# A new order of every engine's tasks, and weight preparation laced with the first image

## The chip, the cores and the metric

The kernel runs on one core of a Trainium2 chip. Its time is in microseconds (us) of the device, from launch to end. The kernel before was timed in 3 runs: median 3233.88, from 3227.86 to 3242.86.

## The reference

Sixteen images x of 512 channels and 32x32 pixels go through self-attention over their 1024 pixels, with 8 heads of width 64:

```python
h = jnp.einsum('oc,bcn->bno', wp, xf)            # wp: 1536x512, rows normalised
qkv = h.reshape(B, N, n_heads, 3 * d_k)
q, k, v = jnp.split(qkv, 3, axis=-1)
q = pixnorm(q) * scale                            # x / sqrt(mean(x*x) + eps)
k = pixnorm(k) * scale
v = pixnorm(v)
attn = jnp.einsum('bihd,bjhd->bijh', q, k)
attn = jax.nn.softmax(attn, axis=2)
res = jnp.einsum('bijh,bjhd->bihd', attn, v)
res = jnp.einsum('oc,bnc->bon', wo, res.reshape(B, N, C))   # wo: 512x512, normalised
return (a_c * x + b_c * res) / div
```

## The kernel before

Every factor of a product is split into a high and a low part, and three products (high-high, high-low, low-high) are summed. Each engine runs one fixed list of tasks, and semaphores count how many tasks of each kind are done. For one image the tasks are:

- TensorE (PE): `project` n = 0..23 (12 matmuls into one of two banks of `ps_dense`), `score` m = 0..31 (12 matmuls, two slots of 128 keys by 512 queries and two heads), `attend` m = 0..31 (48 matmuls, the same two slots into `ps_pv`), `project_out` k = 0..7 (12 matmuls, again a bank of `ps_dense`). A slot is t = 2m or 2m+1; 64 slots make an image, 8 a unit (`take`), 16 a pair of heads.
- ScalarE (ACT): `square` and `copy_proj` of each `project`; `exp` of each slot; `high_probs` of the slots with t % 8 in (1, 4, 6); the high parts of x, v, q and k, and of the result; `finish` of the output.
- VectorE (DVE): `reduce`, `seed_norms`, `scale`; `split_probs_high` of the other 40 slots (line 619) and `split_probs_low` of all 64 (line 628); the low parts; `take_pv`; `add_out`.
- GpSimd (POOL): `norms`, 14 dependent steps for each of 3 groups of `project`.
- SyncE (SP): loads, stores and the transposing DMAs `turn_qk` and `turn_res`, in one queue.

What follows from the buffers: `exp` of slot t needs the scores of t and the low part of slot t-2 (two `e_tile`); the scores of slot t need `exp` t-2 (two slots of `ps_score`); a high part of slot t needs `attend` of slot t-4 (four `probs`), counted by the finished pair of slots (`VISITS`); a matmul group in a bank of `ps_dense` needs the `copy_proj` or `add_out` of the group before it in that bank (`bank_free`). The chain of a slot is score, exp, high part, low part, attend.

The order is a set of hand-over tables: each task has a tick in a period of 4096 ticks, negative or above 4095 where it runs in the period of the image before or after. `timeline` walks the ticks, and only their order on an engine matters. So in one pass of the loop an engine works for three images: late tasks of b-1 (below with a minus, as out0-), those of b, early ones of b+1 (with a plus). Images 1 to 14 are the loop; image 0's early part, and the last two passes, are written out. Before all this stands the preparation of 16 tiles of weights, stage after stage: all 16 loaded and squared, one chain of norms, 16 scaled, then turned on PE, split by ACT and DVE (lines 513 to 526, 700 to 730, 836 to 845).

```python
SCORE_AT = (-42, 56, 141, 572, 697, 817, 936, 1056, ...)
PROB_BUFS = 4
VISITS = SLOTS // 2
```

## Time and profile before

| | us |
|---|---|
| median of the runs shown | 3233.88 (3227.86 to 3242.86) |
| time of the profiled execution | 3256.49 |
| span of its profile, first to last instruction | 3254.4 |
| PE busy in the span | 3027.5 (93%) |
| DVE busy | 2666.0 (82%) |
| ACT busy | 2304.7 (71%) |
| POOL busy | 335.8 (10%) |

The profiled execution is 0.7% longer than the median of the others. Matmuls are pipelined, so that the durations of neighbours overlap: how long a task holds PE is read from the start of one task to the start of the next. "Idle before" is the time in which the engine did nothing before a row, with the instruction that ended it. The clock column is the share of TensorE's full clock that was granted.

### The profile page before, as it was taken

The numbers are of one execution on the slowest core, as the hardware profiler recorded it, in microseconds if no ns is written. First come the engines' busy times: TensorE is split into PE (matmuls) and PEld (weight loads), VectorE is DVE, ScalarE is ACT, GpSimd is POOL, SyncE is SP. The second block draws the span as 40 slices with busy tenths as digits, with TensorE's granted clock in tenths as the row PEclk, the third lists the DMA queues.
The fourth block names the chain that finished last, engine by engine and source line by source line (L and its number), as shares of the span: only waits on it lengthen the run. The fifth ranks groups of instructions, "written<-read, shape, count | busy, mean of one in ns | idle before, by whom it ended". The sixth has DMA issues, their size and how long they took to land.

```text
span 3254.4 us, 91845 instructions
## 1 busy us (share of the span) xinstructions
PE 3027.5 (93%) x36928; PEld 2060.7 (63%) x36928; DVE 2666.0 (82%) x3295; ACT 2304.7 (71%) x2865; POOL 335.8 (10%) x678
## 2 busy tenths in 40 slices
PE   4899999999999899999989999899999999999987
PEld 3666666766667566666666667566665666667653
DVE  3788787888879888797888878788897887878875
ACT  4677676767767777676777767677776776767664
POOL 0120100201102011100201002011010201002010
PEclk9999999999999999999999999999999999999999
DMA  2312323124142321323223232231423223232232
GB/s 78 62 42 49 90 48 92 41 60 94 36 102 44 80 63 38 102 48 83 49 57 90 43 99 36 69 81 35 108 40 83 57 48 91 48 92 41 50 79 59
DMA packets 459635, 212.11 MB, mean 65 GB/s; under 512 B 407953, under 2 KB 407953, under 8 KB 459153
## 3 DMA queue, kind: packets, MB, share of 16 engines
q1 hardware_dynamic: 459152, 205.58, 28.0%
q8 instruction: 315, 5.16, 0.7%
q14 instruction: 168, 1.37, 0.1%
HBM read 71.30 MB, written 33.55 MB: 32 GB/s over the span
## 4 chain that ended last, share of the span: by engine, by line
issue 77%; POOL 10%; PE 5%; DVE 5%; ACT 1%; DMA 1%; POOLq 1%; SPq 0%; DVEq 0%; ACTq 0%
POOL rs L323 3%; POOL rs_t L319 2%; POOL rs_t L317 2%; POOL rs_t L321 2%; DVE probs L628 2%; PE ps_pv L799 1%; DVE probs L619 1%; PE ps_dense L758 1%; PE ps_score L778 1%; PE ps_dense L762 1%; PE ps_dense L760 1%; POOL sumsq L314 1%; ACT e_tile L456 1%; DVE arena L590 0%; ACT probs L463 0%
## 5 line engine op out<-in xcount | busy, mean ns | idle before, releaser
L456 ACT ACTIVATE e_tile<-ps_score,shift 128x1024 f32<-128x1024 f32 x1024 | 1109.3, 1113 | 316.3 <-PE ps_score L778 183.2
L628 DVE TENSOR_TENSOR probs<-e_tile,probs 128x1024 f16<-128x1024 f32 x1024 | 1242.0, 1226 | 56.4 <-ACT probs L463 47.1
L799 PEld LDWEIGHTS ps_pv<-v_pair,probs 128*128 128x128 f16 x24576 | 804.2, 98 | 297.8 <-DVE probs L628 145.6
L799 PE MATMUL ps_pv<-v_pair,probs 128*128 128x65 f16 (+1 forms) x24576 | 863.1, 194 | 119.6 <-DVE probs L628 87.6
L778 PE MATMUL ps_score<-qkT 64*128 64x512 f16 x6144 | 762.1, 381 | 6.8 <-ACT e_tile L456 3.9
L619 DVE CAST probs<-e_tile 128x1024 f16<-128x1024 f32 x640 | 442.2, 693 | 247.2 <-ACT e_tile L456 241.4
L758 PE MATMUL ps_dense<-wpT_hi,x_hi 128*128 128x512 f32 x1536 | 629.9, 410 | 8.4 <-DVE x_lo L557 7.0
L762 PE MATMUL ps_dense<-wpT_hi,x_lo 128*128 128x512 f32 x1536 | 601.9, 392 | 0.0
L760 PE MATMUL ps_dense<-wpT_lo,x_hi 128*128 128x512 f32 x1536 | 600.2, 391 | 0.0
L778 PEld LDWEIGHTS ps_score<-qkT 64*128 64x128 f16 x6144 | 257.6, 95 | 312.7 <-issue 42.6
L416 ACT ACTIVATE squares<-ps_dense 128x512 f32<-128x512 f32 x384 | 228.1, 594 | 277.4 <-PE ps_dense L762 277.4
L463 ACT ACTIVATE probs<-e_tile 128x1024 f16<-128x1024 f32 x384 | 405.9, 1057 | 15.0 <-PE ps_pv L799 0.2
L758 PEld LDWEIGHTS ps_dense<-wpT_hi,x_hi 128*128 128x128 f32 x1536 | 288.7, 188 | 145.8 <-issue 81.6
L566 DVE TENSOR_REDUCE sumsq<-squares 128x8 f32<-128x512 f32 x384 | 261.7, 681 | 103.6 <-ACT squares L416 93.8
L762 PEld LDWEIGHTS ps_dense<-wpT_hi,x_lo 128*128 128x128 f32 x1536 | 288.8, 188 | 64.2
L760 PEld LDWEIGHTS ps_dense<-wpT_lo,x_hi 128*128 128x128 f32 x1536 | 289.7, 189 | 53.1
L314 POOL TENSOR_TENSOR sumsq<-sumsq,shift 128x64 f32<-128x64 f32 x48 | 19.7, 411 | 2761.7 <-DVE rs L534 2761.7
L590 DVE TENSOR_TENSOR arena<-arena,rs 128x1024 f32<-128x1024 f32 x192 | 228.8, 1221 | 34.4 <-POOL rs L325 34.4
L483 ACT ACTIVATE x_res<-x_res 128x512 f32<-128x512 f32 x128 | 80.7, 630 | 244.3 <-DVE x_res L655 244.3
L815 PE MATMUL ps_dense<-resT,woT_hi 128*128 128x512 f16 x512 | 207.0, 404 | 48.6 <-ACT arena L426 44.2
L426 ACT ACTIVATE arena<-ps_dense 128x512 f32<-128x512 f32 x384 | 225.6, 592 | 0.2 <-DVE arena L610 0.2
L816 PE MATMUL ps_dense<-resT,woT_hi 128*128 128x512 f16 x512 | 205.6, 402 | 0.0
(50 smaller groups left out, 1765.7 us busy)
## 6 DMA issues: line engine op xcount, KB each, us to landing
x_raw<-in_x SPq DMA_DIRECT2D x128, 256.0 KB, 3.0
x_res<-in_x SPq DMA_DIRECT2D x128, 256.0 KB, 2.7
out<-x_res SPq DMA_DIRECT2D x128, 256.0 KB, 2.5
arena<-in_w_proj SPq DMA_DIRECT2D x24, 128.0 KB, 2.6
qkT<-arena SPq DMA_TRANSPOSE x128, 4.3
resT<-res_split SPq DMA_TRANSPOSE x128, 3.1
arena<-in_w_out SPq DMA_DIRECT2D x1, 1024.0 KB, 5.7
```

What stands on the lines that cost most here:

```text
L416: act.activation(squares[:, n % 2, :], ps_dense[:, PROJ_BANK[n], :], ACT.Square).then_inc(squared, 1)
L456: act.activation(e_tile[:, t % 2, :, :], ps_score[:, t % 2, :, :], ACT.Exp, bias=shift[:, 0:1], scale=1.0 / (QK_UP * QK_UP)).then_inc(exp_ ...
L463: act.activation(probs_of(b, t, 0), e_tile[:, t % 2, :, :], ACT.Copy).then_inc(probs_high_act, 1)
L566: dve.tensor_reduce(sumsq[:, g, nt, :], squares[:, n % 2, :].rearrange("p (g d) -> p g d", d=D), AX.X, ALU.add).then_inc(reduced, 1)
L590: dve.tensor_tensor(v, v, r, ALU.mult).then_inc(scaled, 1)
L619: dve.tensor_copy(probs_of(b, t, 0), e_tile[:, t % 2, :, :]).then_inc(probs_high, 1)
L628: dve.tensor_tensor(probs_of(b, t, 1), e_tile[:, t % 2, :, :], probs_of(b, t, 0), ALU.subtract).then_inc(probs_low, 1)
L758: pe.matmul(ps_dense[:, bank, :], x_hi[:, ct, pix], wpT_hi[:, ct, cols], start=(ct == 0), stop=False)
L760: pe.matmul(ps_dense[:, bank, :], x_hi[:, ct, pix], wpT_lo[:, ct, cols], start=False, stop=False)
L762: mm = pe.matmul(ps_dense[:, bank, :], x_lo[:, ct, pix], wpT_hi[:, ct, cols], start=False, stop=(ct == CT - 1))
L778: mm = pe.matmul(ps_score[:, t % 2, h, :], k[rows, k_part, :], q[rows, :, q_part, :], start=(i == 0), stop=(i == 2))
L799: mm = pe.matmul(ps_pv[:, h, o:o + n], probs_of(b, t, part)[:, h, queries], v[:, cols], start=(j == 0 and it == 0 and part == 0 and cols.s ...
```

## The change

Three things change, and no operation of an image's work does.

1. All tables of the period are new. On PE one pass of the loop reads, before:

```
attend31- score1 attend0 score2 proj14 proj15 proj16 proj17 proj18 proj19 attend1 score3 proj20 attend2 score4 out0- attend3 score5 out1- attend4 score6 out2- ... (score, dense, attend by turns) ... attend26 score28 attend27 score29 attend28 score30 attend29 score31 attend30 score0+
```

and now:

```
attend29- score31- proj13 score0 attend30- attend31- score1 proj14 proj15 proj16 score2 attend0 attend1 score3 proj17 score4 attend2 proj18 attend3 score5 out0- out1- proj19 attend4 score6 out2- ... proj9+ attend23 score25 proj10+ score26 attend24 attend25 score27 proj11+ score28 attend26 attend27 score29 proj12+ score30 attend28
```

`PROJ_BANK` and `OUT_BANK` swap most banks. The tables of the other engines follow.

2. The weights go through in three chains (tiles 0 to 3, 4 to 7, 8 to 15), and their tasks stand in one list with image 0's early tasks (tables `FIRST_..._AT` and `W_..._AT`). The turned weights use all four banks of `ps_score`, squares two scratch tiles. `first` adds waits for image 0: a projection for the weights it reads, a copy into the arena for the tile it overwrites, the first score for all 16.

3. `pv_done` goes up for each slot, not for each two.

```diff
+W_CHAINS = ((0, 4), (4, 8), (8, 16))
-SCORE_AT = (-42, 56, 141, 572, 697, 817, 936, 1056, 1175, 1300, 1420, 1540, 1659, 1779, 1904, 2029, 2154, 2279,
+SCORE_AT = (19, 56, 248, 278, 829, 866, 988, 1012, 1363, 1379, 1439, 1537, 1643, 1667, 1693, 1854, 1898, 2312,
...
-PROJ_BANK = (0, 1, 0, 1, 0, 1, 0, 1, 0, 1, 0, 1, 0, 1, 0, 1, 0, 1, 0, 1, 0, 1, 0, 1)
-OUT_BANK = (1, 0, 1, 0, 0, 1, 0, 1)
+PROJ_BANK = (1, 0, 1, 0, 1, 0, 1, 0, 1, 0, 1, 0, 1, 0, 1, 0, 1, 0, 1, 0, 1, 0, 1, 0)
+OUT_BANK = (0, 1, 1, 0, 1, 0, 1, 0)
...
+W_TURN_AT = (-4096, -4088, -4080, -4072, -4016, -4008, -4000, -3976, -3968, -3960, -3952, -3904, -3896, -3888,
...
-            body(-1, prev=False, cur=False)
+            for s in range(-span, 0):
+                task(0, s, opening)
             body(0, prev=False)
...
+        def first(b, *others):
+            return isinstance(b, int) and b == 0 and not any(others)
+        def turned_of(m):
+            return ps_score[:, m // 2 % 2, m % 2, :].rearrange("p (t o) -> p t o", o=P)
...
             def copy_proj(b, n):
+                if first(b, n >= RING):
+                    act.wait_ge(w_turned, n + 1)
...
             def high_qk(b, i):
+                if first(b, i):
+                    act.wait_ge(w_turned, W_TILES)
...
             def high_probs(b, t):
-                after(act, pv_done, VISITS * b + (t - PROB_BUFS) // 2 + 1)
+                after(act, pv_done, SLOTS * b + t + 1 - PROB_BUFS)
...
             def split_probs_high(b, t):
                 dve.wait_ge(exp_done, SLOTS * b + t + 1)
-                after(dve, pv_done, VISITS * b + (t - PROB_BUFS) // 2 + 1)
+                after(dve, pv_done, SLOTS * b + t + 1 - PROB_BUFS)
...
+            def norm_weights(c):
+                tiles = W_CHAINS[c]
+                a, y, t = (buf[:, tiles[0]:tiles[1]] for buf in (w_sumsq, w_rs, w_rs_t))
+                dve.wait_ge(w_squared, tiles[1])
...
             def project(b, n):
+                if first(b, nt):
+                    pe.wait_ge(w_low, GROUP_UNITS * (g + 1))
...
             def score(b, m):
+                if first(b, m):
+                    pe.wait_ge(w_low, W_TILES)
...
             def attend(b, m):
-                mm.then_inc(pv_done, 1)
+                    mm.then_inc(pv_done, 1)
...
+            def turn_weights(m):
+                pe.wait_ge(w_scaled, m + 1)
+                after(pe, w_low, m - 3)
+                for ct in range(CT):
+                    mm = pe.transpose(turned_of(m)[:, ct, :], w_raw[:, m, ct * P:(ct + 1) * P], ident32[:, :])
+                mm.then_inc(w_turned, 1)
```

Three places of the lists. First, the start of PE's list: line 840, now 959, turns the weights, and the other rows are the first projection. Before:

```order
L735 UNCONDITIONAL_BRANCH
L840 MATMUL ps_score<-ident,arena 128x128 x64
L758 MATMUL ps_dense<-wpT_hi,x_hi 128x512
L760 MATMUL ps_dense<-wpT_lo,x_hi 128x512
L762 MATMUL ps_dense<-wpT_hi,x_lo 128x512
```

Now:

```order
L864 UNCONDITIONAL_BRANCH
L959 MATMUL ps_score<-ident,arena 128x128 x16
L889 MATMUL ps_dense<-wpT_hi,x_hi 128x512
L891 MATMUL ps_dense<-wpT_lo,x_hi 128x512
L893 MATMUL ps_dense<-wpT_hi,x_lo 128x512
```

Image 0's first projection now stands behind 4 turned tiles (16 matmuls), no longer behind 16.

Second, ACT at the turn from one group of projections to the next, in the last pass. The first fence (before) holds square 20, exp 8 and 9, high 9, the high part of q and k, finish 0, exp 10 and 11, the high part of the result, and copy 20 (line 426), for which out1- waits:

```order
L416 ACTIVATE squares<-ps_dense 128x512
L456 ACTIVATE e_tile<-ps_score,shift 128x1024 x2
L463 ACTIVATE probs<-e_tile 128x1024
L450 ACTIVATE arena<-arena 128x4x256
L483 ACTIVATE x_res<-x_res 128x512
L456 ACTIVATE e_tile<-ps_score,shift 128x1024 x2
L479 ACTIVATE res_split<-res 128x4x128
L426 ACTIVATE arena<-ps_dense 128x512
```

Now out1- waits for copy 18 (line 498, the last row), behind exp 7 and 8, square 17, copy 17, the high part of q and k, square 18, exp 9 and high 9:

```order
L530 ACTIVATE e_tile<-ps_score,shift 128x1024 x2
L486 ACTIVATE squares<-ps_dense 128x512
L498 ACTIVATE arena<-ps_dense 128x512
L524 ACTIVATE arena<-arena 128x4x256
L486 ACTIVATE squares<-ps_dense 128x512
L530 ACTIVATE e_tile<-ps_score,shift 128x1024
L537 ACTIVATE probs<-e_tile 128x1024
L498 ACTIVATE arena<-ps_dense 128x512
```

Between a square and the copy of the same bank stand two tasks, where there were eight.

Third, DVE at the start of the last pass. Before: high and low of slot 0, take 7 (lines 636, 640), low of slot 1, a low part of v, and so on:

```order
L619 CAST probs<-e_tile 128x1024
L628 TENSOR_TENSOR probs<-e_tile,probs 128x1024
L636 RECIPROCAL inv_sum<-ps_pv 128x8
L640 TENSOR_TENSOR res<-ps_pv,inv_sum 128x2x4x64
L628 TENSOR_TENSOR probs<-e_tile,probs 128x1024
L599 TENSOR_TENSOR v_pair<-arena,v_pair 128x4x2x64
```

Now slot 63 of the image before, with the low part of v 0 between its two halves, reduce 11 and 12, the high part of slot 0, low parts of v 1 and 2, of q and k 1, reduce 13, and the low parts of slots 0 and 1:

```order
L715 CAST probs<-e_tile 128x1024
L695 TENSOR_TENSOR v_pair<-arena,v_pair 128x4x2x64
L724 TENSOR_TENSOR probs<-e_tile,probs 128x1024
L662 TENSOR_REDUCE sumsq<-squares 128x8 x2
L715 CAST probs<-e_tile 128x1024
L695 TENSOR_TENSOR v_pair<-arena,v_pair 128x4x2x64 x2
L706 TENSOR_TENSOR arena<-arena 128x4x256
L662 TENSOR_REDUCE sumsq<-squares 128x8
L724 TENSOR_TENSOR probs<-e_tile,probs 128x1024 x2
```

The seam between two images, which held attention alone, now holds dense work's followers among it.

## Rows read from the trace of the kernel before

**Rows 1.** The page: busy time and share of the span of each engine.
```profile
PE 3027.5 (93%) x36928; PEld 2060.7 (63%) x36928; DVE 2666.0 (82%) x3295; ACT 2304.7 (71%) x2865; POOL 335.8 (10%) x678
```

**Rows 2.** Waits of the whole run: engine, line, whom for, us in total, times, longest.
```profile
PE ps_dense L815 <- ACT arena L426: 44.2, 15, 3.0
```

**Rows 3.** Windows: stretch and length, busy us of PE, PEld, DVE, ACT, POOL, clock, DMA.
```profile
1658.00:1855.00 197.00, 188.03 (x2308) 127.64 (x2304) 165.02 (x203) 142.34 (x177) 21.20 (x42) 0.98 0.29 66
```

**Rows 4.** Timeline, PE: start, length; where score 0 of images 0, 1, 15 starts.
```profile
105.78 4.54 PE L778 MATMUL ps_score<-qkT 64*128 64x512 f16 x24 [2.88 <-DMA qkT<-arena]
283.72 1.47 PE L778 MATMUL ps_score<-qkT 64*128 64x512 f16 x12
3035.35 1.47 PE L778 MATMUL ps_score<-qkT 64*128 64x512 f16 x12
```

**Rows 5.** Timeline, PE, from 1720: a score, a projection, attend, score, an output projection, attend.
```profile
1720.39 1.47 PE L778 MATMUL ps_score<-qkT 64*128 64x512 f16 x12
1721.79 0.50 PE L758 MATMUL ps_dense<-wpT_hi,x_hi 128*128 128x512 f32 x1
...
1724.64 1.65 PE L799 MATMUL ps_pv<-v_pair,probs 128*128 128x65 f16 x48
1726.23 1.47 PE L778 MATMUL ps_score<-qkT 64*128 64x512 f16 x12
1727.63 0.39 PE L815 MATMUL ps_dense<-resT,woT_hi 128*128 128x512 f16 x1
...
1730.23 1.63 PE L799 MATMUL ps_pv<-v_pair,probs 128*128 128x65 f16 x48
```

**Rows 6.** Timeline, seam of images 8 and 9; in brackets idle time before, and what ended it.
```profile
1661.91 1.96 PE L799 MATMUL ps_pv<-v_pair,probs 128*128 128x65 f16 x48 [3.00 <-DVE probs L628]
1663.81 2.74 PE L778 MATMUL ps_score<-qkT 64*128 64x512 f16 x12
```

**Rows 7.** Timeline, PE, end of image 0: scores 30 and 31, no dense work between.
```profile
275.90 1.47 PE L778 MATMUL ps_score<-qkT 64*128 64x512 f16 x12
...
280.11 1.47 PE L778 MATMUL ps_score<-qkT 64*128 64x512 f16 x12
```

**Rows 8.** Timeline, PE: the first matmul of out1- and what it waited for.
```profile
1703.38 0.39 PE L815 MATMUL ps_dense<-resT,woT_hi 128*128 128x512 f16 x1 [2.98 <-ACT arena L426]
```

**Rows 9.** Windows with the clock (third column from the end): after seam, inside out1-, plain stretch.
```profile
1663.00:1665.00 2.00, 2.00 (x25) 1.13 (x23) 1.90 (x4) 1.07 (x2) 0.00 (x0) 0.51 0.00 0
...
1725.00:1750.00 25.00, 25.00 (x344) 14.59 (x340) 18.95 (x24) 15.98 (x19) 0.00 (x0) 1.00 0.38 117
1704.00:1707.00 3.00, 3.00 (x8) 1.06 (x7) 0.65 (x1) 0.79 (x2) 0.00 (x0) 0.50 0.02 8
```

**Rows 10.** Groups by line: shapes, count, busy us, mean ns, idle before.
```profile
L628 DVE TENSOR_TENSOR probs<-e_tile,probs 128x1024 f16<-128x1024 f32 x1024 | 1242.0, 1226 | 56.4 <-ACT probs L463 47.1
L456 ACT ACTIVATE e_tile<-ps_score,shift 128x1024 f32<-128x1024 f32 x1024 | 1109.3, 1113 | 316.3 <-PE ps_score L778 183.2 <-DVE probs L628 123.2
L619 DVE CAST probs<-e_tile 128x1024 f16<-128x1024 f32 x640 | 442.2, 693 | 247.2 <-ACT e_tile L456 241.4 <-issue 4.5
```

**Rows 11.** Timeline, the start: first square, first norm step, first turned tile, first projection.
```profile
7.91 0.63 ACT L517 ACTIVATE res<-arena 128x512 f32<-128x512 f32 x1 [5.89 <-DMA arena<-in_w_proj]
...
25.06 0.17 DVE L701 TENSOR_SCALAR w_sumsq<-w_sumsq 128x16 f32<-128x16 f32 x1 [23.75 <-ACT res L517]
...
28.91 1.94 PE L840 MATMUL ps_score<-ident,arena 128*128 128x128 f32 x8 [28.91 <-DVE arena L716]
...
59.94 0.77 PE L758 MATMUL ps_dense<-wpT_hi,x_hi 128*128 128x512 f32 x1 [7.01 <-DVE x_lo L557]
```

**Rows 12.** The page, DMA issues: count, KB each, median us from issue to landing.
```profile
x_raw<-in_x SPq DMA_DIRECT2D x128, 256.0 KB, 3.0
qkT<-arena SPq DMA_TRANSPOSE x128, 4.3
```

**Rows 13.** Timeline, the end: DVE's last add.
```profile
3250.47 0.69 DVE L655 SCALAR_TENSOR_TENSOR x_res<-ps_dense,x_res 128x512 f32<-128x512 f32 x1 [2.69 <-DMA x_res<-in_x]
```

More of the change, by code:

```diff
@@ L268, in probs_of, with timeline @@
             return probs[:, t % PROB_BUFS, part, :, :]
-        def timeline(eng, task):
+        def timeline(eng, task, steady, opening):
             span = SLOTS * TICKS
@@ L325, in norms, with task @@
                 pool.tensor_tensor(y, y, rs_unit[:, g, :, :], ALU.mult).then_inc(norm_step, 1)
-            norm_at = at(NORM_AT)
-            def task(b, s):
-                for g in norm_at.get(s, ()):
+            pool.wait_ge(consts_set, CONSTS)
+            steady = dict(norm=at(NORM_AT))
+            opening = dict(norm=at(FIRST_NORM_AT))
+            def task(b, s, when):
+                for g in when["norm"].get(s, ()):
                     norms(b, g)
-            pool.wait_ge(consts_set, CONSTS)
-            timeline(pool, task)
+            timeline(pool, task, steady, opening)
         @block.sync
@@ new lines, in high_weights @@
+            def high_weights(m):
+                act.wait_ge(w_turned, m + 1)
+                if m < WP_TILES:
+                    act.activation(wpT_hi[:, :, m * P:(m + 1) * P], turned_of(m), ACT.Copy).then_inc(w_high, 1)
+                else:
+                    o = (m - WP_TILES) * P
+                    act.activation(woT_hi[:, :, o:o + P], turned_of(m), ACT.Copy, scale=WO_UP).then_inc(w_high, 1)
+            act.wait_ge(consts_set, CONSTS)
+            steady = dict(exp=at(EXP_AT),
+                          cast=at(HIGH_P_AT),
+                          square=at(SQUARE_AT),
+                          copy=at(COPY_AT),
+                          high_v=at(HIGH_V_AT),
+                          high_qk=at(HIGH_QK_AT),
+                          high_res=at(HIGH_RES_AT),
+                          finish=at(FINISH_AT),
+                          high_x=at(HIGH_X_AT))
@@ L493, in task @@
+            def task(b, s, when):
+                if when is opening:
+                    for m in when["w_square"].get(s, ()):
+                        square_weights(m)
+                    for m in when["w_high"].get(s, ()):
+                        high_weights(m)
+                for t in when["exp"].get(s, ()):
                     exp(b, t)
-                for t in cast_at.get(s, ()):
+                for t in when["cast"].get(s, ()):
                     if t % UNIT_SLOTS in ACT_HIGH:
@@ L519, in _ @@
-            for m in range(W_TILES):
-                act.wait_ge(w_turned, m + 1)
-                turned = ps_score[:, m % 2, 0, :].rearrange("p (t o) -> p t o", o=P)
-                if m < WP_TILES:
-                    act.activation(wpT_hi[:, :, m * P:(m + 1) * P], turned, ACT.Copy).then_inc(w_high, 1)
-                else:
-                    o = (m - WP_TILES) * P
-                    act.activation(woT_hi[:, :, o:o + P], turned, ACT.Copy, scale=WO_UP).then_inc(w_high, 1)
-            act.wait_ge(consts_set, CONSTS)
@@ L528, in _ @@
-            timeline(act, task)
+            timeline(act, task, steady, opening)
         @block.vector
@@ L735, in _ @@
+            timeline(dve, task, steady, opening)
         @block.tensor
@@ new lines, in _ @@
+            pe.wait_ge(ident_made, 2)
+            pe.wait_ge(consts_set, CONSTS)
+            steady = dict(score=at(SCORE_AT),
+                          attend=at(ATTEND_AT),
+                          proj=at(PROJ_AT),
+                          out=at(OUT_AT))
+            opening = dict(score=at(FIRST_SCORE_AT),
+                           attend=at(FIRST_ATTEND_AT),
+                           proj=at(FIRST_PROJ_AT),
+                           out=at(FIRST_OUT_AT),
+                           w_turn=at(W_TURN_AT))
@@ L826, in task @@
+            def task(b, s, when):
+                if when is opening:
+                    for m in when["w_turn"].get(s, ()):
+                        turn_weights(m)
+                for m in when["attend"].get(s, ()):
                     attend(b, m)
-                for m in score_at.get(s, ()):
+                for m in when["score"].get(s, ()):
                     score(b, m)
-                for n in proj_at.get(s, ()):
-                    project(b, n, s)
-                for k in out_at.get(s, ()):
-                    project_out(b, k, s)
@@ L846, in _ @@
-            timeline(pe, task)
+                for n in when["proj"].get(s, ()):
+                    project(b, n)
+                for k in when["out"].get(s, ()):
+                    project_out(b, k)
+            timeline(pe, task, steady, opening)
 _INS = {"x": "x", "L0_conv_w_proj": "w_proj", "L0_conv_w_out": "w_out"}
```

358 lines of the change are left out of this document (212 added, 146 removed), and 18 rows, old and new, of tables (EXP_AT, HIGH_P_AT, LOW_P_AT).

## The prediction, made before the changed kernel ran

> **What bounds the kernel now.** I read the page first: PE is busy 93% of the span, DVE 82%, ACT 71% [rows 1]. POOL and the DMA queues stand far below. So PE sets the end where it works, and what an order can give is PE's lost time, plus the ends of the program where PE has no work.
>
> Next come the positions of score 0 of each image on PE's timeline [rows 4]. Image 0 reaches it at 105.8, image 1 at 283.7, image 15 at 3035.4, and the span ends at 3254.4. The middle 14 periods last (3035.35 - 283.72) / 14 = 196.5 us each. They repeat almost to the microsecond, so one of them can be read for all.
>
> How much of a period is work? Busy time overcounts pipelined matmuls, so I take the distance from the start of one task to the start of the next [rows 5]: a score 1.40, a projection 2.85, an attend 1.59, an output projection 2.60. Inside the batch of six projections the distance is 2.72. Per image: 32 x 1.40 = 44.8; 24 projections at 2.72 to 2.95, 67.5; 32 x 1.57 = 50.2; 8 x 2.60 = 20.8; together about 183.5 us. So a period loses 196.5 - 183.5 = 13 us. The window of image 8 shows 197.0 - 188.0 = 9.0 of it as idle PE [rows 3]; the other 4 are matmuls at a lower clock.
>
> Where in the period do the 13 us lie?
> - **The seam between images.** In the tables before, attend 27 to 31 and score 29 to 31 of one image and score 0 to 2 and attend 0 of the next stand without one dense task between. PE needs 1.40 + 1.57 = 3.0 for such a pair, but scores 30 and 31 start 4.2 apart [rows 7]. Two slots take DVE 2 x 1.23 for low parts and some 0.9 for high ones, and an `exp` of 1.11 must end before each high part [rows 10]; with two e_tile that chain wants more than PE's 3.0. In the steady middle one dense task of 2.6 to 2.9 stands in each pair, the pair takes 5.6 to 5.9, and the chain is hidden. At the seam attend31- finally waits 3.00 for DVE, and the clock drops to 0.51 just behind it, to 1.2 GHz, so that score 1 takes 2.7 for 1.4 [rows 6, 9]. I count 0.9 to 1.3 for each of attend 28, 29 and 30 and 4.5 around attend 31 with the slow score: 7.5.
> - **out1-.** It waits 2.98 for copy 20 of its bank [rows 8], 15 times [rows 2]; the clock is 0.50 inside it [rows 9], which adds 1.4. Together 4.4.
> - **attend 19**, the rest: about 1.
>
> One rule of the Trainium skill measures this otherwise: "Perfetto Trace Analysis", Identifying the Most-Contended Engine, says that matmul busy time does not show how near TensorE is to its roofline, and that the share of weight loads does. That share is 63% [rows 1], so by the page a third could be gained; by the starts of rows 5 no order comes below 183.5 a period, since the loads of a task stand in its distance already.
>
> **The change, part by part.** The terms are against the profiled execution, 3256.5; it is 0.7% above the median of the runs, so the sum is scaled by 3233.9/3256.5 at the end.
>
> *Period, work.* The counts of tasks stay. The new list has 4 places where a projection follows a projection, where there were 6, and 16 where a score follows one, where there were 6; against that 16 attends are followed by an attend or a dense task, at 1.49 in place of 1.57. By these distances the work is 183.7. Nothing gained, nothing lost. (The same page, Matmul Optimizations, asks that matmuls run back to back in batches, because the engine's power follows its use. That speaks against taking the batch of six apart. The window 1725 to 1750, with single dense tasks between scores and attends and no idle time, has clock 1.00 [rows 9]: by the row the price is the 0.2 above, by the rule it would be a lower clock somewhere that no row here shows.)
>
> *Period, waits.* I laid the new lists side by side, with the durations of rows 5 and 10 and 0.1 for each hand-over, and followed each wait. A slot's chain from score to attend needs some 5 to 6 us when its neighbours' tasks stand in it. PE's work between score m and attend m was 3.0 for pairs 28 to 31 and 0, 5.8 for five others and 8.2 or more else; now it is nowhere below 5.6 and mostly 7 to 17. So the waits at attend 28 to 31 go. What comes late next, place by place:
>  - *Seam.* score31-, then proj13, score 0, attend30-, attend31-, score 1, proj14. proj14 waits for copy 12 of its bank; copy 12 waits for the low part of v 2, because it overwrites that place of the ring; this stands on DVE behind low 63-, two reduces, the high part of slot 0 and v 1. I get copy 12's end at 12.5 us after the start of attend29-, and PE free at 11.7: 0.9 lost. The rest of the seam has room: attend31-'s second slot needs low 63- at 9.5, and it is there at 8.8.
>  - *out0-, out1-.* Their banks are freed by copies 17 and 18, which ACT does at once. PE is there at 38.4 and 41.0, copy 18 ends at 38.9. No wait. The price moves to DVE, which stands at add1- for 1.4 and at add3- for 1.2, its list having them as pairs; scores 6 and 8 stay 1 to 2 us ahead. DVE's 165.0 busy of 197 [rows 3] leaves 19 idle in a period of 184, so it can pay.
>  - *Third pair of heads.* attend 16 waits for low v 5, behind scale 8 to 11 and three reduces: 0.4. proj4+ waits for copy 2, behind the high part of q and k 6: 0.1.
>  - *x loads.* load 4 and 5 of the next image are issued behind store6-, at 98.7; with 3.0 to landing [rows 12] ACT's high part, due at 100.8, waits 1 us, with exp 30 and copy 22 behind it. copy 22 then meets proj0+ within 0.3.
>
>  Sum 1.4 on PE that I can name, and about 1 for places within 0.3 of a wait. No idle stretch is long like that of rows 6, so I take the full clock. Period: 183.7 + 2.3 = 186.0, a gain of 10.5. Bounds: 183.9 with nothing more than 0.2 lost; above, a DVE that never catches up (rival A). Over 14 periods: 147.
>
>  *`pv_done` per slot.* It frees a probs buffer 0.8 earlier for even slots and costs one semaphore step more; it is part of the walk above and gets no term of its own.
>
>  *Image 0's period* (105.8 to 283.7, 177.9) has no output projections: 183.5 - 20.8 = 163 of work, and pairs without dense work where the chain shows. Those stay. Only the seam goes: 5 gained, between 0 and 8.
>
>  *Start.* Before: first square at 7.9, norms at 25.1 when all 16 are squared, first turned tile at 28.9, projections only at 59.9 [rows 11], score 0 at 105.8. Now two x pieces are issued first, so group 0 is there at about 9; four squares of 0.82, 12.3; 15 norm steps of 0.21, 15.5; scales and turned tiles, then high and low of tile 3, about 22: the first projection. From there PE has 13 x 2.72 + 12 x 0.97 = 47 more before proj13, plus some 3 at the low clock and 2 for copies behind ACT's squares: the last tile is turned at 73. Its end releases the high part of q and k (1.05), the low part (1.2) and the transpose, 4.3 [rows 12]: score 0 at 80. ACT and DVE have about 40 and 45 of work in those 73 and are not the bound. Gain 25. Below 15 it falls if ACT's one list (squares of weights between the squares of projections) holds the banks back by 1 us at each projection; above 28 it cannot rise, since PE's own work is 51 of the 73.
>
>  *End.* The last pass loses the seam of image 14 and out1-: 7 of the 12, as the outputs of 14 are still there. From attend 14 on it is attention without dense work, bound by the chain, and stays. After attend 31 before, 35 us with the eight outputs, last add at 3250.5 [rows 13]; now turn_res 7 stands behind store 1, but loads of x for the residual stand one place sooner: about 31. Gain 11, between 3 and 15.
>
>  Sum: 147 + 5 + 25 + 11 = 188. 3256.5 - 188 = 3068.5; scaled, 3047 us.
>
> **The rivals.**
> A. *DVE becomes the bound.* Its list holds 166 of a period of 186, and a wait on DVE at a paired add holds up every low part behind it. For: 247 us idle at the high parts are waits for exp that a tighter PE does not remove [rows 10]; several places have under 1 us of room. Against: PE's lookahead has doubled nearly everywhere. If each of some five tight places costs 1 more, the period is 190.5 to 191: 14 x 5.7 = 80, 3 at image 0, 20 at the start, 6 at the end, 109: 3125.
> B. *Nothing slips.* Period 183.9: 14 x 12.6 = 176, with 7, 28 and 14: 225 gained, 3010.
> C. *The gain is only the start*: new waits of 7 to 11 at the seam, because 16 tasks of two images meet there: 14 x 3 = 42, with 25: 3165.
> D. *Slower.* SP is one queue. Loads x 4 and 5 stand behind store6-, which waits for finish6-; behind the high part of x 4 ACT holds exp 30, copy 22 and so proj0+ and all scores after 16. Each us that the load lands late is one on PE. At 15 us a period the kernel is as before, above 16.5 it is slower by over 0.5%: 14 x 3.5 = 49 lost less 29 at the ends, 3254. Against it: a landing of 3.0 in the median, and ACT has the whole stretch from 94 to 100 in front of it.
> E. *The new start does nothing*, because SP's list holds load_x 2 (it waits for the split of piece 0) ahead of weight group 1. That wait ends at about 6.5, before the issues of group 0 are through; by this the rival costs nothing, and if it did, 10 of the 25.
>
> **How the numbers follow.** Forecast, with all that lies from 3010 to 3085: 0.70. A, 3085 to 3135: 0.18. B, below 3010: 0.05. C: 0.04. D: 0.01, and 0.02 for the case between C and D, in which new waits eat all but 0.5%. The range leaves out most of B, C, D and the upper end of A, together about 0.17: 3008 to 3125. A measurement of this kernel tells apart about 0.5%. Faster by over that 0.97, within it 0.02, slower 0.01.
>
> **What the profile after would show.** Score 0 of image 0 near 80 and successive ones 186 apart; no idle PE above 1.5 us at the seam, the out projection's wait for copy gone from the waits; PE's busy share at 97 to 98%; the clock at 0.99 or more outside start and end; copy 12 as the releaser of one dense task per image. Wrong would be: periods of 190 and more (A), a DMA of x as a releaser on ACT of over 3 us (D), score 0 of image 0 after 90 (the start).

## The result, and the profile after

| | before | after |
|---|---|---|
| median of the runs, us | 3231.79 (4 runs) | 3158.49 (4 runs) |
| span of the profile, us | 3254.4 | 3151.6 |
| mean granted clock in the span | 0.983 | 0.990 |

The ratio is 0.9766, with a 95% interval from 0.9738 to 0.9793. The forecast was 3047 us, a ratio of 0.942, with a range of 3008 to 3125. So the direction was right and the size was not: the changed kernel is 2.3% faster, where 5.8% was forecast, and its time lies 33 us above the range. (One of the four runs of the hinted kernel below took 4165.1 us at a mean granted clock of 0.655, where its other three had 0.996 to 0.997; its ratio is taken without that slow run.)

The page, busy time of each engine (before: [rows 1]):

```profile
PE 2997.7 (95%) x36928; PEld 2029.7 (64%) x36928; DVE 2686.7 (85%) x3325; ACT 2293.5 (73%) x2865; POOL 503.2 (16%) x678
```

The positions of score 0 of images 0, 1 and 15 on PE's timeline of after. They answer to [rows 4]; columns are start, length, engine and line, operation, and in brackets the idle time before with what ended it:

```profile
71.75 3.70 PE L911 MATMUL ps_score<-qkT 64*128 64x512 f16 x16 [4.45 <-DMA qkT<-arena]
...
241.16 1.47 PE L911 MATMUL ps_score<-qkT 64*128 64x512 f16 x12
...
2944.39 1.47 PE L911 MATMUL ps_score<-qkT 64*128 64x512 f16 x12
```

These give the four terms of the forecast one by one. The start gained 105.8 - 71.8 = 34.0 (forecast 25). Image 0's period gained 177.9 - 169.4 = 8.5 (forecast 5). The end, from score 0 of image 15, gained 219.0 - 207.2 = 11.8 (forecast 11). But the 14 middle periods last (2944.39 - 241.16) / 14 = 193.1 for 196.5. They gained 3.45 each, 48 in all, where 10.5 each, 147 in all, was forecast. The sum is 102.7 between the two traces. Between the medians it is 73: the profiled execution of before, 3256.5, was longer than all four runs of the table, and that of after was the shortest of its four.

So the whole miss is in the period. A window from one score 0 to the next, in after and, in the second fence, in the hinted kernel of the experiments below, which has the same tasks (columns as in [rows 3]: stretch, length, busy us of PE, PEld, DVE, ACT, POOL, clock, DMA share, GB/s):

```profile
1786.49:1979.22 192.73, 186.22 (x2306) 126.61 (x2306) 165.99 (x202) 141.37 (x176) 31.95 (x42) 0.99 0.31 67
```

```profile
1735.12:1921.59 186.47, 184.86 (x2305) 125.63 (x2305) 166.36 (x203) 141.87 (x177) 31.91 (x42) 1.00 0.31 69
```

In after PE is idle for 6.5 us of this period, 1.6 in the hinted kernel, and its busy time is 1.4 longer for the same matmuls. Both lie in one place, the seam. The start of each matmul can be set against the start of the same matmul in the hinted kernel. With 150 matmuls on either side of score 0 taken as the seam, after loses there, over 13 seams, 4.5 us ahead of score 0 and 2.6 behind it, and nothing (-0.05) in the rest of the period. PE's timeline at the seam of images 8 and 9 (the attend rows are attend28-, attend29-, attend30- with half of attend31-, and the other half of attend31-; the score rows are score31-, 0 and 1; matmuls of proj13 and proj14 are left out):

```profile
1774.41 1.64 PE L932 MATMUL ps_pv<-v_pair,probs 128*128 128x65 f16 x48
1779.01 1.88 PE L932 MATMUL ps_pv<-v_pair,probs 128*128 128x65 f16 x48 [2.95 <-DVE probs L724]
1780.82 2.74 PE L911 MATMUL ps_score<-qkT 64*128 64x512 f16 x12
...
1786.49 1.57 PE L911 MATMUL ps_score<-qkT 64*128 64x512 f16 x12
1787.99 2.38 PE L932 MATMUL ps_pv<-v_pair,probs 128*128 128x65 f16 x72
1791.75 0.91 PE L932 MATMUL ps_pv<-v_pair,probs 128*128 128x65 f16 x24 [1.38 <-DVE probs L724]
1792.59 1.47 PE L911 MATMUL ps_score<-qkT 64*128 64x512 f16 x12
1795.37 0.50 PE L889 MATMUL ps_dense<-wpT_hi,x_hi 128*128 128x512 f32 x1 [1.31 <-ACT arena L498]
```

The rows 1779.01, 1791.75 and 1795.37 wait 5.6 us together. (The window above holds the last two and, at its end, the next wait of the first kind, 2.99.) The clock just behind the first, and for comparison in a stretch with no idle PE (windows, the clock is the third column from the end):

```profile
1779.00:1783.00 4.00, 4.00 (x60) 2.47 (x60) 1.66 (x2) 0.68 (x1) 0.00 (x0) 0.65 0.43 71
...
1725.00:1750.00 25.00, 25.00 (x386) 17.98 (x384) 22.38 (x28) 19.80 (x23) 11.00 (x14) 1.00 0.22 34
```

The first row puts PE's 2.95 down to DVE's low part (line 724). Is that right? DVE's timeline, line 724 in low 59, 60, 61 and 62, and the last row high 63:

```profile
1774.68 1.23 DVE L724 TENSOR_TENSOR probs<-e_tile,probs 128x1024 f16<-128x1024 f32 x1
...
1777.02 1.22 DVE L724 TENSOR_TENSOR probs<-e_tile,probs 128x1024 f16<-128x1024 f32 x1
...
1779.44 1.22 DVE L724 TENSOR_TENSOR probs<-e_tile,probs 128x1024 f16<-128x1024 f32 x1
1786.21 1.22 DVE L724 TENSOR_TENSOR probs<-e_tile,probs 128x1024 f16<-128x1024 f32 x1 [5.55 <-ACT probs L537]
1789.26 0.69 DVE L715 CAST probs<-e_tile 128x1024 f16<-128x1024 f32 x1 [1.82 <-PE ps_pv L932]
```

It is not. attend29- needs slots 58 and 59, and low 59 ended at 1775.9, before PE became free at 1776.05. The trace's records of the sequencers, which no busy time counts, show what PE did: its COMPARE_BRANCH, the branch at the end of the loop's body, runs from 1775.46 to 1778.83. ACT's timeline at the same place, exp 62 and high 62, has a wait "for nothing that the profile shows":

```profile
1782.32 1.11 ACT L530 ACTIVATE e_tile<-ps_score,shift 128x1024 f32<-128x1024 f32 x1 [3.52 <-PE ps_score L911]
1785.12 1.06 ACT L537 ACTIVATE probs<-e_tile 128x1024 f16<-128x1024 f32 x1 [1.69 <-issue]
```

ACT's sequencer issues its branch at 1782.43 and comes back at 1784.94, 2.5 later. DVE's branch is issued at 1786.36, and the next instruction is there at 1789.05, 2.7 later. PE's branch takes 3.4 to 3.8 in after's 13 ways back, and 0.08 at the fourteenth, where the loop is left.

That gave **theory L**. Each way back of the loop stops its engine's sequencer for some 3 us, and in the new order the three stops lie one behind the other on one path: PE's holds up score31-, which holds up exp 62; ACT's holds up high 62 behind it; DVE's holds up high 63 behind that; attend31-, copy 12 and proj14 wait at the end. In before the three stops fell nearly together: ACT's from 1656.9 to 1659.4, PE's from 1657.9 to 1661.7, DVE's from 1658.9 to 1662.0. So the 3.00 in front of attend31- [rows 6] ended when PE's branch did. (By the positions of score 0 this is the seam of images 7 and 8, not of 8 and 9.) But here the low part that the row names, low 63-, had ended only at 1661.1, some 0.65 before the branch: without the branch most of this wait would stand.

### The profile page after: what moved, and what is told of

Read it like the earlier page. It is cut to its first block, busy times and chain, and to the rows that moved or that the text cites. A ratio compares the mean times of both kernels' runs of the same rounds, so it can differ in the third digit from the quotient of the medians.

```text
span 3151.6 us, 91554 instructions
## 1 busy us (share of the span) xinstructions
PE 2997.7 (95%) x36928; PEld 2029.7 (64%) x36928; DVE 2686.7 (85%) x3325; ACT 2293.5 (73%) x2865; POOL 503.2 (16%) x678
## 4 chain that ended last, share of the span: by engine, by line
issue 72%; POOL 16%; PE 5%; DVE 4%; ACT 1%; DMA 1%; POOLq 1%; SPq 0%; DVEq 0%; ACTq 0%
POOL rs_t L371 4%; POOL rs L375 3%; POOL rs_t L373 3%; POOL rs_t L369 3%; POOL sumsq L366 2%; DVE probs L724 1%; PE ps_pv L932 1%; PE ps_score L911 1%; PE ps_dense L889 1%; PE ps_dense L893 1%; PE ps_dense L891 1%; DVE probs L715 1%; ACT e_tile L530 1%; POOL rs L377 0%; DVE arena L686 0%
## 5 line engine op out<-in xcount | busy, mean ns | idle before, releaser
L530 ACT ACTIVATE e_tile<-ps_score,shift 128x1024 f32<-128x1024 f32 x1024 | 1133.8, 1112 | 443.9 <-PE ps_score L911 288.5
L932 PEld LDWEIGHTS ps_pv<-v_pair,probs 128*128 128x128 f16 x24576 | 789.9, 98 | 232.1 <-issue 143.7
L932 PE MATMUL ps_pv<-v_pair,probs 128*128 128x65 f16 (+1 forms) x24576 | 839.7, 194 | 81.0 <-DVE probs L724 51.3
L911 PE MATMUL ps_score<-qkT 64*128 64x512 f16 x6144 | 770.8, 383 | 23.9 <-ACT e_tile L530 19.0
L715 DVE CAST probs<-e_tile 128x1024 f16<-128x1024 f32 x640 | 450.4, 704 | 82.6 <-ACT e_tile L530 41.5
L366 POOL TENSOR_TENSOR sumsq<-sumsq,shift 128x64 f32<-128x64 f32 x48 | 48.9, 1018 | 2499.2 <-DVE rs L630 2499.2
L948 PE MATMUL ps_dense<-resT,woT_hi 128*128 128x512 f16 x512 | 195.4, 382 | 3.7 <-DVE x_res L751 3.7
L949 PE MATMUL ps_dense<-resT,woT_hi 128*128 128x512 f16 x512 | 194.8, 380 | 0.0
L950 PE MATMUL ps_dense<-resT,woT_lo 128*128 128x512 f16 x512 | 194.7, 380 | 0.0
```

The lines of the kernel that those rows point to most:

```text
L530: act.activation(e_tile[:, t % 2, :, :], ps_score[:, t % 2, :, :], ACT.Exp, bias=shift[:, 0:1], scale=1.0 / (QK_UP * QK_UP)).then_inc(exp_ ...
L715: dve.tensor_copy(probs_of(b, t, 0), e_tile[:, t % 2, :, :]).then_inc(probs_high, 1)
L911: mm = pe.matmul(ps_score[:, t % 2, h, :], k[rows, k_part, :], q[rows, :, q_part, :], start=(i == 0), stop=(i == 2))
L932: mm = pe.matmul(ps_pv[:, h, o:o + n], probs_of(b, t, part)[:, h, queries], v[:, cols], start=(j == 0 and it == 0 and part == 0 and cols.s ...
```

## The experiments

**The loops written out, in after and in before.** The loop over images 1 to 14 is replaced by 14 bodies, on PE, ACT, DVE and POOL; nothing else changes (SP had no loop).

```diff
-            if eng is nc.sync:
+            if True:
                 for b in range(1, B - 1):
                     body(b)
```

> The changed kernel with its 14 middle passes written out on every engine, no loop. Theory L (the loop's way back): in the changed kernel's trace each engine's sequencer stands between its COMPARE_BRANCH and the next instruction: about 3.8 us on PE, 2.55 on ACT, 2.75 on DVE, once a period, and these stops follow one another there through score31, exp 62, low 62, attend31. Then the period falls from 193.3 to 184 to 187, and the time from 3158 to about 3060 (3045 to 3090). Theory S (the seam's own chain of score, exp, high, low is too long, whatever the branch does): under 20 us are gained, 3140 or more.

Measured: 3061.82 us, ratio to before 0.9438 (0.942 to 0.9457). The middle periods last 186.44, where the forecast had 186.0. A window of about one period:

```profile
1725.00:1911.00 186.00, 184.48 (x2303) 124.96 (x2302) 165.89 (x202) 141.60 (x177) 31.49 (x42) 1.00 0.30 69
```

> The kernel before with its 14 middle passes written out on every engine. Theory L: in the trace of before the three stops fall together (ACT's branch at 1656.9, PE's at 1657.9, DVE's at 1658.9), so they cost 3.0 to 4.5 us a period with the slow clock behind them, 13 times: 40 to 60 us, time about 3180. My prediction's reading (the 3.00 us at attend31- are the chain of attention without dense work): under 15 us.

Measured: 3230.82 us, ratio 0.9961 (0.9946 to 0.9976), so 13 us of gain, 0.9 a period; between the two traces, of which that of before is a long one, it is 1.8 (196.54 - 194.73). Here theory L's number, 3180, was wrong: it had counted what the stops last, and the chain of the slots, which ended only 0.65 before PE's branch did, takes most of it back. PE's timeline of this seam (the first two rows are attend31-, the last one half of attend 0):

```profile
1647.55 0.91 PE L799 MATMUL ps_pv<-v_pair,probs 128*128 128x65 f16 x24 [1.10 <-DVE probs L628]
1648.68 0.92 PE L799 MATMUL ps_pv<-v_pair,probs 128*128 128x65 f16 x24 [0.23 <-DVE probs L628]
1649.53 1.47 PE L778 MATMUL ps_score<-qkT 64*128 64x512 f16 x12
1651.70 0.90 PE L799 MATMUL ps_pv<-v_pair,probs 128*128 128x65 f16 x24 [0.70 <-DVE res L640]
```

The 3.00 and the score of 2.74 [rows 6] are gone; waits of 1.10, 0.23 and 0.70 for DVE stand there instead. The loop costs after 6.65 a period (193.09 - 186.44) and before 1.8. The difference, 4.8, is what the new order lost to it.

**One engine's loop at a time.** In the first kernel PE is written out and ACT, DVE and POOL keep their loops; in the second only PE keeps its loop.

```diff
-            if eng is nc.sync:
+            if eng is nc.sync or eng is nc.tensor:
```

> The changed kernel with the passes written out on PE (and SP, as before) alone; ACT and DVE keep their loop at the seam. Theory L with the stops in a row: PE's stop of 3.1 goes, ACT's and DVE's 1.7 to 1.9 each remain on the path to attend31- and copy 12: period about 188 to 190, time about 3100. If one engine's stop were all, this would already give the 3060 of the version without any loop.

```diff
-            if eng is nc.sync:
+            if eng is not nc.tensor:
```

> The changed kernel with a loop on PE alone; ACT, DVE and POOL are written out. With PE written out alone the period was 189.7, with all 186.4, with the loop on all 193.1. If the stops stand in a row on one path, PE's is worth what its removal gave, 3.4: period 189.5 to 190. If ACT's and DVE's stops only cost because PE's comes ahead of them, the period is 186.4 + 3.0 or less, and the sum of single costs would not reach 6.65.

Measured: 3108.77, ratio 0.9583 (0.9559 to 0.9608), periods of 189.71; and 3118.66, ratio 0.9616 (0.9575 to 0.9658), periods of 190.50. So ACT's and DVE's stops cost 189.71 - 186.44 = 3.3 a period and PE's 4.1, just above its forecast. Together they cost 6.65, nearly the sum of 7.4: they do not hide each other, as stops in a row would not. Set against the hinted kernel as above, PE's loop alone loses 4.5 ahead of score 0 and 0.1 behind it, the other loops alone nothing ahead and 3.3 behind. No kernel parts ACT's stop from DVE's. After's rows show 1.69 in front of high 62 and 1.82 in front of high 63, 3.5 in all, so that both seem to count.

**The loop's end moved.** A pass begins some third of an image later (tick 1537 to 1694 of 4096), where by the forecast PE's stop alone would be felt; the order of the tasks is the same.

```diff
+CUTS = (1537, 1561, 1694, 1537, 0)
...
-                with eng.Fori(1, B - 1) as b:
-                    body(b)
+                with eng.Fori(1, B - 2) as b:
+                    turn(b)
```

> The changed kernel, same order of tasks, same loop of one image, but the place where the loop's pass ends and begins is moved from the seam to the middle of the output projections: PE before score 11, ACT before exp 22 (where it was idle for 2.97 us anyway), DVE before the high part of slot 23 (idle 1.73). 13 passes in the loop, not 14. Theory L: PE's own stop stays, about 3 us a period, those of ACT and DVE fall into idle time: period 187, time about 3080 (3065 to 3105). Theory S: the seam costs what it did, 3150 or more.

Measured: 3116.83, ratio 0.9608 (0.9576 to 0.964), periods of 190.21 for about 187. The seam loses nothing any more against the hinted kernel's (-0.2), and 4 us a period are lost elsewhere. The move gains less than theory L gave it, and the trace says why. PE now has no data to wait for behind the branch, so its stop stands alone, and it is longer than at the seam: the branch takes 4.4 to 6.4 here. PE's waits show it as "issue", idle time for which nothing of the profile is the reason (engine, line, whom for, us in total, times, longest):

```profile
PE ps_score L926 <- issue: 29.7, 12, 3.8
```

**What is the stop?** Three kernels tell the price of a branch from the price of what it jumps to. The first keeps the loops, POOL's too, and gives each a hint for its last branch as the first instruction of every pass.

```diff
-                with eng.Fori(1, B - 1) as b:
+                with nc.Fori(1, B - 1, engines=[eng.engine], hint_back_edge=True) as b:
```

> The changed kernel, its loops kept, but each of the three engines' loops (PE, ACT, DVE) arms a hint for the branch at its end with the first instruction of every pass, so that the sequencer can fetch the code of the loop's head before it gets there. Theory L (the stops at the loop's end, 3.8 us on PE and 2.5 to 3 on ACT and DVE, are the fetch of code that lies far back): the stops shrink to under 0.7 us, the period goes from 193.1 to about 187, and the time to about 3070 (3060 to 3085), ratio to the kernel before 0.943 to 0.951. Rival F (the stop is the price of a branch and of the reload of registers, whatever is fetched): no change, 3150 to 3165, ratio 0.974 to 0.979. Rival G (the hint fetches only a part of what is missing, so half of each stop is left): 3100 to 3125.

Measured: 3065.48, ratio 0.9436 (0.9389 to 0.9484), periods of 186.68. PE's branch takes 0.36, for 3.4 to 3.8. The page and PE's first waits of this kernel; in after the second of these stood at 51.3:

```profile
PE 2978.7 (97%) x36928; PEld 2022.4 (66%) x36928; DVE 2687.0 (88%) x3325; ACT 2292.2 (75%) x2865; POOL 502.2 (16%) x678
```

```profile
PE ps_score L911 <- ACT e_tile L530: 14.7, 29, 1.4
...
PE ps_pv L932 <- DVE probs L724: 8.9, 24, 1.1
```

The seam of the same two images, PE's timeline: score31-, score 0, attend30- and attend31- in one piece, score 1, proj14:

```profile
1730.78 1.47 PE L911 MATMUL ps_score<-qkT 64*128 64x512 f16 x12
...
1735.12 1.47 PE L911 MATMUL ps_score<-qkT 64*128 64x512 f16 x12
1736.53 3.12 PE L932 MATMUL ps_pv<-v_pair,probs 128*128 128x65 f16 x96
1739.58 1.47 PE L911 MATMUL ps_score<-qkT 64*128 64x512 f16 x12
1741.78 0.50 PE L889 MATMUL ps_dense<-wpT_hi,x_hi 128*128 128x512 f32 x1 [0.74 <-ACT arena L498]
```

This is the seam that the prediction had walked through: no wait at attend31-, 0.74 at proj14 for copy 12 (forecast 0.9), no score at the low clock.

The second is the written-out kernel with short loops put in.

```diff
+                if 1 <= b < B - 1 and eng in (nc.tensor, nc.scalar, nc.vector):
+                    with eng.Fori(0, 4):
+                        eng.wait_ge(w_low, W_TILES)
```

> The changed kernel written out as in after_unrolled; at the start of each of images 1 to 14 PE, ACT and DVE each go through a loop of 4 passes that holds only a wait for the weights, which was met long ago: 3 branches back over a few instructions, on three engines, 14 times. Theory L (a stop is the fetch of far code; a jump back over a few instructions is cheap): each branch costs 0.1 to 0.3 us, hidden or nearly so: within 15 us of after_unrolled (3062), 3055 to 3080. Rival F (each taken branch costs 2.5 to 3.8 us wherever it goes): 3 x 3.8 = 11.4 us on PE in each of 14 images and as much on the chain behind it: 3062 + 160 = 3220 or more.

Measured: two runs of 3076.24 and 3109.72, at mean granted clocks of 0.997 and 0.938, ratio 0.9522 (0.9446 to 0.9598). The first lies in theory L's range, the second and the median of 3092.98 above it. The trace, of the first, has periods of 187.38, 0.9 above the version without these loops. Three jumps back and one way out are done in 1.2 us on PE, a jump back taking 0.21. Rival F wanted 11.4 a period; a jump over a few instructions does not stop the sequencer for microseconds. The same stands in after itself: POOL's loop, 42 operations to a pass, has its next instruction 0.17 behind the branch. The spread of the two runs leaves open whether the small price is 0.9 or more.

The third has two images in a pass.

```diff
-                with eng.Fori(1, B - 1) as b:
+                with eng.Fori(1, B - 1, 2) as b:
                     body(b)
+                    body(b + 1)
```

> The changed kernel with two images to a pass of the loop, 7 passes for 14. Theory L (6.65 us for each way back, nothing for the body's length): 7 ways back are left, 3062 + 7 x 6.65 = 3108 (3098 to 3118), and images alternate between periods of about 186.4 and 193. Rival H (what is lost in the loop is spread over the body, in code fetched again at every pass, and not in the way back): near 3158, all periods alike.

Measured: 3122.9, ratio 0.9614 (0.9565 to 0.9663), periods alternating between 189.6 and 193.6. Both are off: theory L's 3108, and rival H's even periods. A pair of images takes 383.0, 10 more than two of 186.4, where one way back was to cost 6.65. The shorter periods hold a part of it: DVE's branch comes just behind score 0 (1389.69, score 0 at 1389.36), so its stop counts into the period that then begins. Set against the hinted kernel as above, the seam with the way back loses 6.2 ahead of score 0 and 2.7 behind it, the seam in the middle of a pass nothing (-0.2), and the rest of a period 0.7. So nearly all is the way back, and of rival H 0.7 a period at most is left. The way back costs more than in after because PE's branch takes 4.5 to 5.0 here, for 3.4 to 3.8.

The three fit one reading: the stop is the fetch of code that lies far from the branch. The Trainium skill has this rule in "Runtime: NRT & Kernel Launch", Instruction fetch mechanics: a taken branch to a target outside the two blocks held by the sequencer forces a fetch before anything executes. The Trainium skill's "Advanced Engine Details and Errata", Control Flow Timing, gives about 108 ns for a compare-and-branch. PE's takes 0.08 here where a loop is left, 0.21 over a few instructions, and for these bodies 3.4 to 3.8.

The trace has the fetches themselves. The page's rows of the instruction queues (packets, MB, share), in after, hinted, and written out:

```profile
q8 instruction: 315, 5.16, 0.7%
q14 instruction: 168, 1.38, 0.1%
```

```profile
q8 instruction: 303, 4.96, 0.7%
q14 instruction: 92, 0.75, 0.1%
```

```profile
q8 instruction: 290, 4.75, 0.6%
q14 instruction: 87, 0.71, 0.1%
```

Queue 8 follows PE's loop: 315 packets where PE alone has one, 290 where PE alone is written out. Queue 14 follows the others' (87 and 168). A packet of queue 8 is 16 KB, and the loop brings 25 more of them for 13 ways back. In each of after's 13 stops of PE one such packet starts 1.0 to 1.4 us behind the branch, and it lasts 0.94 to 1.31; the stop ends some 1.4 us behind it. In the two-image kernel there are two in each stop, which overlap and last 1.1 to 2.4. At the moved place the last packet starts only 1.9 to 3.0 behind the branch; why it comes late is open. So these stops are longer because their fetches end later. Length of the jump alone does not do it, since the moved place has the same length and the longest stops. In the 0.36 of the hinted branches no packet of queue 8 starts.

**proj20 late, in before.** To size the term of out1- alone, proj20 with its square and copy goes behind the first outputs, and the banks of the outputs swap.

```diff
 PROJ_AT = (..., 417, 479,
-    604, 1207, 1810, 1936)
+    1100, 1207, 1810, 1936)
...
-OUT_BANK = (1, 0, 1, 0, 0, 1, 0, 1)
+OUT_BANK = (0, 1, 0, 1, 0, 1, 0, 1)
```

> The kernel before, but projection 20 stands behind out3- instead of ahead of out0-, its square, copy and reduce follow, and the output banks are (0, 1, 0, 1, ...). So out1- no longer needs copy 20, which ACT reaches eight tasks late. My term for this place: 2.98 us of wait and 1.4 at the lower clock, 4.4 a period, 15 times: 66 us, about 3170 against a before of 3235. Rival (PE only comes earlier to a wait that exists anyway, at the outputs or the seam): under 25 us.

Measured: 3191.1, ratio 0.9836 (0.9803 to 0.9869), a gain of 53 us, 3.4 to 3.8 a period (the trace has 192.52 for 196.54, 4.0). Of PE's waits for line 426's copy [rows 2] nothing over 1.0 is left. The term of 4.4 was right in kind and some 0.5 to 1 too large, and the time missed the forecast of about 3170 by 21, a part of it because before's own median had risen to 3243. This small edit of before alone is worth 1.6%, where the whole change brought 2.3%.

**The weights first again, in after.** One chain of 16 tiles ahead of image 0, in the new kernel.

```diff
-W_CHAINS = ((0, 4), (4, 8), (8, 16))
+W_CHAINS = ((0, 16),)
...
```

Behind the dots the tables of the weights' and of image 0's first tasks move accordingly.

> The changed kernel's order of the period, but the weights prepared as before: all 16 tiles loaded, squared, one chain of norms, scaled, turned and split, and only then image 0's first tasks in their new order. It undoes part 2 of the change alone. Score 0 of image 0 stood at 105.8 before and at 71.8 after. If the lacing gave that, it comes back to 100 to 108 and the time grows by 30 to 36 us against the changed kernel; if the new order of image 0's own tasks gave a part, it grows by less than 25.

Measured: 3184.16, ratio 0.9818 (0.9776 to 0.986), so 17 us above after by the ratios, whose intervals overlap: the size is unclear by the times, and the following is from single traces. Its score 0 starts at 96.6, 24.8 behind after's 71.8; its span is 31 longer, of which 7 are middle periods of 193.6 for 193.1, for which no reason is known. So of the start's 34 the three chains bring 25, and the new order of image 0's own first tasks the other 9 (before: 105.8), which the forecast had not split off.

**Finished slots counted one by one, in before.**

```diff
-                after(act, pv_done, VISITS * b + (t - PROB_BUFS) // 2 + 1)
+                after(act, pv_done, SLOTS * b + t + 1 - PROB_BUFS)
...
-                mm.then_inc(pv_done, 1)
+                    mm.then_inc(pv_done, 1)
```

> The kernel before with pv_done counted for each slot, part 3 of the change alone, old order. I gave it no term: within 0.3% of before. Rival: the earlier release of a probs buffer (0.8 us) shortens the chain at the seam, where attention stands alone: 1 to 2 us a period, 15 to 30 us.

Measured: 3251.55, ratio 1.002 (1.0001 to 1.0038). In the old order it gains nothing by itself and costs 0.4% at most, as the prediction had it. The new order without it was not tried.

## Why the prediction was right or wrong, point by point

- **The failed step is "Period, waits".** The walk through the new lists took tasks alone, "with 0.1 for each hand-over". The way back of the loop is no task, so it was in neither list, and it falls just at the seam. Without it the forecast holds: 186.44 for 186.0 a period, and a ratio of 0.9438 (hinted 0.9436) for 0.942. Some of this closeness is luck. The period without stops has 1.5 idle where 2.3 of waits were forecast, and 184.9 for the 183.7 of work; in the whole time, the start gained 9 more than forecast. With the loop a period costs 6.65 more, 93 us over 14. That is nearly all of the 99 between 147 and 48.
- **"No idle stretch is long like that of rows 6, so I take the full clock"** fell with it: 2.95 idle in front of attend29-, a score of 2.74 for 1.40 behind it, a clock of 0.65 over 4 us. Without the stops the clock is 1.00 in the window of a period.
- **The wait at attend31- in before** was read as all chain, and mostly that holds: the trace's row named DVE, PE's branch had stood there for 3.8, but it ended only 0.65 behind the chain. So the error in the sum is not this row. Without the loop before gains only 1.8 a period, since the three stops lay side by side and chain waits of 2 us stay. The change made of three stops side by side three in a row.
- **out1-**: right in kind; its wait is gone in after, and it was worth 3.4 to 4.0 for the 4.4 taken, measured in the old order.
- **Other places of the period**, averaged over the periods of after: copy 12 keeps proj14 waiting 1.30 (0.74 hinted; forecast 0.9), attend16 waits 0.2 (0.4), the load of x 0.5 on ACT (1), DVE at add1- 0.9 (1.4). At add3- DVE waits 3.9, for the residual's load, where 1.2 was forecast for another reason; PE does not feel it.
- **The start** gained 34, above the 28 that it "cannot" exceed. The first projection came as forecast (20.9 for 22). From there to the last turned tile PE took 43 for 51. I had a turned tile at 0.97, from the two that stand alone in [rows 11], and they take 0.5 between projections; a part of what PE "cannot" do faster was thus too large. And I had added 3 for a low clock, while the window of this stretch shows 1.00:

```profile
20.90:63.90 43.00, 41.27 (x200) 33.94 (x200) 28.97 (x71) 25.72 (x59) 4.30 (x14) 1.00 0.17 56
```

- **The end** gained 11.8 for 11, image 0's period 8.5 for 5, just outside its 0 to 8.
- **The rivals.** A's time is closer than the forecast's, and the sign it was to be known by, periods of 190 and more, came; but its mechanism is not there: PE's waits on DVE sum to less in the unrolled kernel than in before. C's numbers came nearest: 3165 for 3158, and new waits of 7 at the seam for a gain of 3 a period. But its reason, 16 tasks of two images meeting there, is refuted by the kernels without the stops, whose seam has the same tasks. D and E did nothing: SP's queue cost ACT 0.5, and the start gained. The chance of 0.04 for C was too small because all rivals were made of tasks, as the forecast was.
- **The Trainium skill's advice to batch matmuls** ("Perfetto Trace Analysis", Matmul Optimizations), weighed in the prediction: without the stops the clock of a period with single dense tasks is 1.00, so the row's reading stands. The Trainium skill's other rule weighed there (same page, Identifying the Most-Contended Engine) names the share of weight loads beside a second measure, the FLOPs reached, which this case did not work out. By the share alone a third could be gained; but in the written-out kernel PE is busy for 184.5 of 186 us with weight loads at 125.0, so with this set of matmuls an order has under 1% of a period left.

## What to carry to other kernels

Before an order of tasks is costed, find where the loop's body ends in it on each engine, read in the sequencers' records how long the branch stands there, and put that into the walk as a task of its own; three stops that now lie side by side can come to lie in a row. A loop whose body is long should have its branch hinted, or be written out: here either is worth 3% on top of the change, and in the old order, whose stops lay side by side, writing out gave 0.4%. And a releaser that was done before the engine became free is not what it waited for.

## What the runs showed of the hardware beyond that

A jump back over a body of some 2300 matmuls stopped PE's sequencer at the seam for 3.3 to 4.2 us over all kernels with that loop, over two such bodies for 4.5 to 5.0, at the moved place for 4.4 to 6.4. At the seam ACT's stood for 2.4 to 2.7 and DVE's for 2.7 to 3.1. With the hint PE's took 0.36 to 0.39.

GpSimd's steps depend on what DVE does beside them. POOL's busy time rose from 335.8 [rows 1] to 503.2 for the same 678 instructions. POOL's timeline in after, the first steps of a chain of norms, and then DVE's in the same stretch:

```profile
1803.22 1.21 POOL L366 TENSOR_TENSOR sumsq<-sumsq,shift 128x64 f32<-128x64 f32 x1 [52.94 <-DVE rs L630]
1804.51 0.62 POOL L369 TENSOR_TENSOR rs_t<-rs 128x64 f32<-128x64 f32 x1
1805.21 0.65 POOL L371 TENSOR_TENSOR rs_t<-rs_t,sumsq 128x64 f32<-128x64 f32 x1
1805.94 0.29 POOL L373 TENSOR_TENSOR rs_t<-rs_t,shift 128x64 f32<-128x64 f32 x1
1806.31 1.28 POOL L375 TENSOR_TENSOR rs<-rs_t,rs 128x64 f32<-128x64 f32 x1
```

```profile
1803.06 1.22 DVE L724 TENSOR_TENSOR probs<-e_tile,probs 128x1024 f16<-128x1024 f32 x1
1804.19 0.79 DVE L715 CAST probs<-e_tile 128x1024 f16<-128x1024 f32 x1
1804.90 0.78 DVE L695 TENSOR_TENSOR v_pair<-arena,v_pair 128x512 f16<-128x512 f32 x1
1805.60 0.67 DVE L662 TENSOR_REDUCE sumsq<-squares 128x8 f32<-128x512 f32 x1
1806.20 2.47 DVE L724 TENSOR_TENSOR probs<-e_tile,probs 128x1024 f16<-128x1024 f32 x2
```

A POOL step of 128x64 takes 0.29 beside a reduce, and otherwise ends 0.1 to 0.2 behind the DVE operation beside which it began: 1.2 to 1.3 beside a low part of probs, 0.6 to 0.7 beside a high one or a low part of v. The Trainium skill, "SBUF — State Buffer", SBUF: two separate sides, says that the port pair of the two engines is held for a whole instruction, against a GpSimd operation that reads SBUF, by a DVE operation with two SBUF inputs or in a 2-port mode. The rows agree for the low parts, which have two inputs, and for the reduce, which has one; that the high part's cast is in such a mode no row shows. The scaling waits at most 1.5 at a time for POOL, 45 us in the whole run (34.4 in before), and none of PE's waits names it; whether it costs PE anything no run tried apart.
